# Spreading 24 of 32 expert gathers and sums over the first six head pairs of the next attention

## What is computed

```python
# layer 2: each token goes to its two best experts; their results are weighted and summed
topk_vals, topk_idx = jax.lax.top_k(xf @ router_w.T, 2)
topk_w = jax.nn.softmax(topk_vals, axis=-1)
y = (expert_out_of_each_pair * topk_w).sum(axis=1)
x = x + jnp.tanh(g_ffn[2]) * y
# layer 3: 16 heads over all 512 tokens of a batch, on the normalised x; kv from the context
q_big = rope(einsum(q_hk, w_kc_q)); q_r = einsum(q_big, W_qr); k_r = einsum(rope(kv_c), W_kr)
attn = softmax(q_r k_r^T)            # no scaling
ctx_c = attn @ rope(kv_c); out = (ctx_c @ w_kc_kv^T) @ Wo^T
x = x + jnp.tanh(g_xattn[3]) * out
```

## Time and profile before

| what | us |
|---|---|
| median of 3 runs | 4484.85 (4482.78 to 4489.41) |
| the profiled execution, whole | 4486.73 |
| its span in the trace | 4485.0 |
| PE busy | 3742.6 (83%) |
| DVE busy | 2221.7 (50%) |
| ACT busy | 1204.9 (27%) |
| POOL busy | 363.3 (8%) |

### The profile page before, as it was taken

The page is one execution under the profiler, slowest core; times in us unless marked ns, Lnnn a source line. Parts: engine busy times, 40 slices in busy tenths (PEclk is TensorE's granted clock), DMA queues, the critical chain, the costliest instruction groups (busy, mean ns, idle before and its releaser), DMA issues.

```text
span 4485.0 us, 38317 instructions
## 1 busy us (share of the span) xinstructions
PE 3742.6 (83%) x11794; PEld 1726.6 (38%) x11795; DVE 2221.7 (50%) x3419; ACT 1204.9 (27%) x2333; POOL 363.3 (8%) x388
## 2 busy tenths in 40 slices
PE   2198989884475888937994899999999998999999
PEld 0043434342142444414562344444444443444443
DVE  7787878316365766621113566566665563111111
ACT  1101010013032666612221334434344332001010
POOL 6000000000002222122113000000000000000000
PEclk6599999996786999968997999999999999999999
DMA  2221212130004434234555000000000001222221
GB/s 90 81 75 53 74 56 71 56 123 37 3 0 76 66 50 63 25 142 129 162 164 204 32 32 22 32 32 32 31 22 32 32 22 45 73 80 84 68 87 51
DMA packets 77498, 292.25 MB, mean 65 GB/s; under 512 B 10440, under 2 KB 11336, under 8 KB 66252
## 3 DMA queue, kind: packets, MB, share of 16 engines
q1 hardware_dynamic: 69072, 265.17, 20.1%
q0 software_dynamic: 8320, 25.71, 1.8%
HBM read 256.73 MB, written 33.59 MB: 65 GB/s over the span
## 4 chain that ended last, share of the span: by engine, by line
PE 61%; issue 22%; DVE 7%; DMA 4%; POOL 3%; ACT 2%; SPq 1%; DVEq 0%; POOLq 0%; ACTq 0%
PE BM L338 6%; PE BR L338 6%; PE BS L349 6%; PE BM L1721 5%; PE BM L1772 5%; PE BR L1780 4%; PE BS L1756 3%; PE BM L1731 2%; PE BT L1059 2%; PE BR L1414 2%; PE BM L1403 2%; PE BR L1403 2%; PE BT L1765 2%; PE BM L1745 2%; PE BS L1049 2%
## 5 line engine op out<-in xcount | busy, mean ns | idle before, releaser
L349 PE MATMUL BS<-AR 128*128 128x512 f32 x1024 | 452.8, 595 | 31.9 <-DVE X L393 31.9
L338 PE MATMUL BM<-XT,AR 128*128 (+1 forms) x1024 | 462.8, 595 | 11.9 <-ACT XT L238 5.5
L338 PE MATMUL BR<-XT,AR 128*128 (+1 forms) x1024 | 460.3, 592 | 0.0
L385 DVE TENSOR_TENSOR AR<-AR,BR 128x512 f32<-128x512 f32 x128 | 87.9, 687 | 506.0 <-PE BR L338 494.9
L1944 DVE SCALAR_TENSOR_TENSOR X<-BR,AR,X 128x512 f32<-128x512 f32 x256 | 192.0, 750 | 230.7 <-PE BR L1780 221.4
L1831 ACT COPY AR<-BM 128x512 f32<-128x512 f32 x340 | 199.4, 587 | 397.4 <-PE BM L1772 182.3
L349 PEld LDWEIGHTS BS<-AR 128*128 128x128 f32 x1024 | 191.9, 190 | 287.5 <-issue 229.6
L366 ACT ACTIVATE AR<-BM 128x512 f32<-128x512 f32 x128 | 76.4, 597 | 833.5 <-PE BM L338 833.4
L338 PEld LDWEIGHTS BM<-XT,AR 128*128 128x128 f32 x1024 | 194.5, 191 | 258.3 <-issue 258.3
L338 PEld LDWEIGHTS BR<-XT,AR 128*128 128x128 f32 x1024 | 194.6, 190 | 244.9 <-issue 244.9
L1837 ACT ACTIVATE AR<-BS,AR 128x512 f32<-128x512 f32 x256 | 175.6, 690 | 411.1 <-DVE AR L1931 411.1
(11 more groups left out here) (304 smaller groups left out, 5095.1 us busy)
## 6 DMA issues: line engine op xcount, KB each, us to landing
AR<-l_w_dram SPq DMA_DIRECT2D x128, 512.0 KB, 3.5
AR<-l_wq_dram SPq DMA_DIRECT2D x32, 1152.0 KB, 5.1
AR<-l_w_dram SPq DMA_DIRECT2D x42, 768.0 KB, 4.8
AR<-w2h SPq DMA_DIRECT2D x16, 1024.0 KB, 4.8
QS<-qx SPq DMA_DIRECT2D x32, 512.0 KB, 17.8
AR<-l_w_dram SPq DMA_DIRECT2D x16, 1024.0 KB, 4.8
AR<-l_w_dram SPq DMA_DIRECT2D x8, 1408.0 KB
made<-AR SPq DMA_DIRECT2D x40, 256.0 KB, 4.8
```

What stands on the lines that cost most here:

```text
L338: last = nc.tensor.matmul(bank.rearrange("p (a n) -> p a n", a=1), w[:, kt, a, :], XT[:, ds(b & 1, 1), kt, :], start=kt == 0, stop=kt == K ...
L349: last = nc.tensor.matmul(bank, f.HIDDEN[:, u, st * P:(st + 1) * P], f.DOWN[:, u, :], start=u == 0, stop=u == f.units - 1)
```

## The change

The first four gathers and sums, and the four behind them, stay where they are (k = 0 to 7, batch 0), and POOL issues four more gathers (k = 8 to 11) into the freed buffers ahead of its norm. The gathers k = 12 to 31 go to the beginning of POOL's part of the attention. The sums k = 8 to 31 go into the DVE's loop over pairs, four behind `sums(p)` for p = 0 to 5. To keep the buffers alive the attention's area begins 4 * D columns later, WT0, WT1, YP0 and YP1 get storage of their own, and PROBT3 shrinks to one buffer for both heads; so the context of head 0 moves ahead of the turn of head 1, in the ring's numbering, on PE and on ACT.

```diff
--- before.py
+++ after.py
@@ -1310,8 +1310,10 @@
         EC = a(E + 16 + TW)
         TOK = a(B * ST).bitcast(I32)
         n128 = B * ST * E
-        MX0, MX1, MS, EX, WT0, WT1, POS0, POS1 = [a(B * ST) for _ in range(8)]
-        IDX0, IDX1, YP0, YP1 = [a(B * ST).bitcast(I32) for _ in range(4)]
+        MX0, MX1, MS, EX, POS0, POS1 = [a(B * ST) for _ in range(6)]
+        IDX0, IDX1 = [a(B * ST).bitcast(I32) for _ in range(2)]
+        WT0, WT1 = [sb(n, [P, B * ST])[:, :] for n in ("WT0", "WT1")]
+        YP0, YP1 = [sb(n, [P, B * ST], I32)[:, :] for n in ("YP0", "YP1")]
         NTL, END0, END1, START = a(E), a(E), a(E), a(E)
         EXF = a(TW)
         EXPERT, SLOTS = a(TW).bitcast(I32), a(TW).bitcast(I32)
@@ -1446,6 +1448,21 @@
                     nc.scalar.copy(EHT[:, u, 0:2 * P], bank[:, 0:2 * P])
                     nc.scalar.copy(EHT[0:I - 2 * P, u, 2 * P:], bank[0:I - 2 * P, 2 * P:EK * P]).then_inc(es.free, 1)
 
+        def moe_combine(v, k):
+            tile, j = divmod(k, 2)
+            v.wait_ge(yg_in[k % 4], 16 * (k // 4) + 16)
+            nc.vector.scalar_tensor_tensor(out=X[:, tile, :], in0=YG[k % 4], scalar=(WT0, WT1)[j][:, tile:tile + 1],
+                                           in1=X[:, tile, :], op0=ALU.mult, op1=ALU.add).then_inc(yg_used, 1)
+            v.wait_ge(yg_used, k + 1)
+
+        def moe_gather(pool, k):
+            tile, j = divmod(k, 2)
+            if k >= 4:
+                pool.wait_ge(yg_used, k - 3)
+            nc.gpsimd.indirect_dma_start(out=YG[k % 4], out_offset=None, in_=made,
+                                         in_offset=bass.IndirectOffsetOnAxis(ap=(YP0, YP1)[j][:, tile:tile + 1], axis=0))\
+              .then_inc(yg_in[k % 4], 16)
+
         def moe_vector(v):
             r, m = Count(), Count()
             one = lambda t, n: t.rearrange("p (t o) -> p t o", o=1).to_broadcast([P, B * ST, n])
@@ -1539,12 +1556,8 @@
                     v.wait_ge(y_ready, i * 2 + u + 1)
                     v.sem_inc(er.free, 1)
             l3_context(v)
-            for k in range(2 * B * ST):
-                tile, j = divmod(k, 2)
-                v.wait_ge(yg_in[k % 4], 16 * (k // 4) + 16)
-                nc.vector.scalar_tensor_tensor(out=X[:, tile, :], in0=YG[k % 4], scalar=(WT0, WT1)[j][:, tile:tile + 1],
-                                               in1=X[:, tile, :], op0=ALU.mult, op1=ALU.add).then_inc(yg_used, 1)
-                v.wait_ge(yg_used, k + 1)
+            for k in range(8):
+                moe_combine(v, k)
             v.sem_inc(x_done, B)
             norm_vector(v, 0)
             T_V.step(KT)
@@ -1580,13 +1593,8 @@
                 pool.wait_ge(xg_in[u], (NT // 2 + 1) * 16)
             pool.wait_ge(er.full, ROUTE_R + 2 * NT)
             pool.wait_ge(et.free, NT + 3)
-            for k in range(2 * B * ST):
-                tile, j = divmod(k, 2)
-                if k >= 4:
-                    pool.wait_ge(yg_used, k - 3)
-                nc.gpsimd.indirect_dma_start(out=YG[k % 4], out_offset=None, in_=made,
-                                             in_offset=bass.IndirectOffsetOnAxis(ap=(YP0, YP1)[j][:, tile:tile + 1], axis=0))\
-                  .then_inc(yg_in[k % 4], 16)
+            for k in range(12):
+                moe_gather(pool, k)
             norm_pool(pool)
 
 
@@ -1616,11 +1624,11 @@
         RQ = [a(3, S), a(3, S)]
         QRT = a(S)
         assert a.here() <= E * KT * 2 * I + 2 * EK * D
-        a = area(E * KT * 2 * I + 2 * EK * D)
+        a = area(E * KT * 2 * I + 2 * EK * D + 4 * D)
         MIX = a(3, S)
         QHK, CC3 = [a(S), a(S)], [a(S), a(S)]
         KRT = a(S)
-        PROB3, PROBT3 = [a(ST, S), a(ST, S)], [a(ST, S), a(ST, S)]
+        PROB3, PROBT3 = [a(ST, S), a(ST, S)], a(ST, S)
         SUM3, RS3, NEG3 = [a(2, 2 * ST).rearrange("p u (h s) -> p u h s", h=2) for _ in range(3)]
         KV_TMP = QB.rearrange("p a k n -> p (a k n)").rearrange("p (t c) -> p t c", c=C)
 
@@ -1645,12 +1653,13 @@
                         put("o", "b2", p + 1, h)
                         for k in range(2):
                             put("m", "b", p + 1, h, k)
+                    if p >= 0 and h == 1:
+                        put("m", "ctx", p, 0)
                     if p >= 0:
                         for lt in range(ST):
                             put("t", "turn", p, h, lt)
                 if p >= 0:
-                    for h in range(2):
-                        put("m", "ctx", p, h)
+                    put("m", "ctx", p, 1)
                     if p % 8 == 6:
                         for kt in range(KT):
                             put("t", "norm", p // 8, kt)
@@ -1769,7 +1778,7 @@
                 bank = take(("ctx", p, h))
                 for lt in range(ST):
                     pe.wait_ge(t_free, L3["turn", p, h, lt] + 3)
-                    last = nc.tensor.matmul(bank, KVN[:, p // 8 * ST + lt, :], PROBT3[h][:, lt, :], start=lt == 0, stop=lt == ST - 1)
+                    last = nc.tensor.matmul(bank, KVN[:, p // 8 * ST + lt, :], PROBT3[:, lt, :], start=lt == 0, stop=lt == ST - 1)
                 last.then_inc(m_full, 1)
 
             def outputs(p, h):
@@ -1812,9 +1821,10 @@
                 for h in range(2):
                     if more:
                         big_queries(p + 1, h)
+                    if h:
+                        context(p, 0)
                     turn_probs(p, h)
-                for h in range(2):
-                    context(p, h)
+                context(p, 1)
                 if p % 8 == 6:
                     turn_norm(p // 8)
                 if more:
@@ -1840,7 +1850,7 @@
             def probs(p, h, lt):
                 job = ("turn", p, h, lt)
                 act.wait_ge(t_full, L3[job] + 1)
-                nc.scalar.copy(PROBT3[h][:, lt, :], BT[:, L3[job] % 2, :]).then_inc(t_free, 1)
+                nc.scalar.copy(PROBT3[:, lt, :], BT[:, L3[job] % 2, :]).then_inc(t_free, 1)
 
             def big(p, h, k):
                 if p:
@@ -1880,10 +1890,10 @@
                 if more:
                     for k in range(2):
                         big(p + 1, 1, k)
+                take(("ctx", p, 0), CC3[0])
                 for lt in range(ST):
                     probs(p, 1, lt)
-                for h in range(2):
-                    take(("ctx", p, h), CC3[h])
+                take(("ctx", p, 1), CC3[1])
                 if p % 8 == 6:
                     for kt in range(KT):
                         job = ("norm", p // 8, kt)
@@ -1971,6 +1981,9 @@
                     last = nc.vector.tensor_scalar(XN[:, st, :], X[:, 4 * b + st, :], MV[:, st, 0:1], RSTD[:, st:st + 1], ALU.subtract, ALU.mult)
                 last.then_inc(xn_ready, 1)
 
+            def combine(k):
+                moe_combine(v, k)
+
             v.wait_ge(rope_in, 16)
             for h in range(2):
                 rotate(0, h)
@@ -1984,6 +1997,9 @@
                     for h in range(2):
                         rotate(p + 1, h)
                 sums(p)
+                if 8 + 4 * p < 2 * B * ST:
+                    for k in range(8 + 4 * p, 12 + 4 * p):
+                        combine(k)
                 if p % 8 == 4:
                     norm_begin((p // 8 + 1) % B)
                 if p % 8 == 5:
@@ -1992,6 +2008,8 @@
             add_outputs(NP3 - 1, 1)
 
         def l3_pool(pool):
+            for k in range(12, 2 * B * ST):
+                moe_gather(pool, k)
             for b in range(B):
                 norm_pool(pool)
 
```

## The result

| | before | after |
|---|---|---|
| median of the runs | 4484.61 us (4482.78 to 4489.41, 4 runs) | **4446.2 us** (4444.31 to 4452.07, 4 runs) |
| the profiled execution | 4486.73 | 4444.31 |
| its span | 4485.0 | 4442.6 |

The ratio is 0.9915 with a 95% interval of 0.9898 to 0.9932: 30 to 46 us faster. I had said 4453, between 4447 and 4465. (The runs of experiments 1 and 9 make it ten of this kernel, with a median of 4447.3, so 0.8 us is less than these medians can tell.)

A forecast was written before the change was run, and what follows sets the result against it. PE was taken to stand for XN behind 24 sums that batch 0 does not need. Terms: -34.7 + 0.3 + 3.1 - 1.0 = -32.3 from 4484.85 gives 4452.6, said as 4453, range 4447 to 4465.

The forecast's parts named there:

- The bound: Between experts and last attention, PE waits 31.9 us for XN; with 24 sums moved, PE's own chain comes last instead.
- The norm transposes: PE's turn of XN before the first query matmul: 3.2 us on a busy PE instead of 4.43.
- The weights of pair 0: Their load before the first query: landing at 2424.0 instead of 2428.4 without the gathers, ahead of 2426.0, so no bound.
- The moved sums: DVE in pairs 0 to 5: four sums take 3.11 us of 6.22 idle; only 0.3 us lost, at p = 4.
- crowded-DVE rival: Pairs 0 to 5: sums keep a 1.81 us pace, four take 7.2 us; 6 us lost in all, 4459; 5%.
- The one PROBT3: All pairs: context 0 waits about 0.1 us for its bank, 31 x 0.1 = 3.1 us lost, between 0 and 10.9.
- The slower rivals: PROBT3's single buffer costs 0.35 us a pair (4461, 12%), 0.8 to 1.1 (3%), or 1.8 (4506, 3%).
- The seam held by DMA: Rival before the first query: pair-0 weights land as late as before, start 2428.7, 2.7 us less gain, 4456; 10%.
- The folds: PE's preparation before the KVN transposes: fold loads land in 4.2 us, all later work 1.5 us earlier, at most 2.0.
- The last pair: Context 0 fills PE's 1.36 us wait for the second head's exponentials: 1.0 us gained, between 0 and 2.

The follow-up runs named there:

- experiments 1 and 9: The changed kernel unaltered, run again: 4446.8 us in 1, 2072.0 us from the attention's first load to the end in 9, which also reran before (2107.1 us).
- experiment 6: Changed kernel with eight sums behind each of the first three pairs instead of four behind each of six: median 4476.9 us, ratio 0.9982.
- experiment 3: Changed kernel with the 24 sums in one block behind the norm of batch 0, ahead of the first rotation: median 4471.6 us, ratio 0.9956.
- order-only kernel: Kernel of before with one PROBT3 and context 0 ahead of head 1's turn, gathers and sums unmoved: median 4487.3 us, ratio 1.0004.
- experiment 1: The changed kernel once more, unaltered: median 4446.8 us, ratio 0.9915.

## Why the prediction was right or wrong

Split at S, at the first query, at pair 1's and pair 30's first scores and at the last output, means of two profiles of before and three of the changed kernel:

| stretch (us) | before | after | difference | predicted |
|---|---|---|---|---|
| S to the first query | 83.0 | 47.5 | -35.5 | -34.7 |
| first query to pair 1 | 68.3 | 67.1 | -1.2 | +0.1 |
| pair 1 to pair 30 | 1162.0 | 1164.7 | +2.7 | +3.2 |
| pair 30 to the last output | 83.8 | 80.9 | -2.9 | -0.9 |
| the feed-forward behind it | 710.2 | 710.9 | +0.7 | 0 |
| sum | 2107.2 | 2071.1 | **-36.2** | **-32.3** |

(Each stretch runs from start to start.) The same split by PE's own work, from the windows view, over the stretches where the clock isn't full throughout:

| stretch | PE busy, us | PE idle, us | granted clock |
|---|---|---|---|
| first fold to the first KVN transpose | 22.7, then 19.0 | 9.5, then 10.2 | 0.74, then 0.87 |
| first query to pair 1 | 56.3, then 55.1 | 12.0, then 12.0 | 0.89, then 0.92 |
| pair 30 to the last scores' end | 52.3, then 51.7 | 6.9, then 6.8 | 0.93, then 0.94 |
| from there to the last output's end | 21.2, then 20.2 | 4.0, then 2.8 | 0.86, then 0.93 |

Of the first and the last of these stretches, the rows of the first profiles, before and then after (columns of the earlier trace rows):

```profile
2390.09:2421.57 31.48, 22.16 (x33) 7.87 (x33) 15.02 (x17) 8.78 (x15) 15.99 (x15) 0.76 0.80 278
2383.15:2411.44 28.29, 17.84 (x33) 6.37 (x33) 14.93 (x23) 8.78 (x15) 9.71 (x9) 0.92 0.78 265
...
3750.34:3775.43 25.09, 21.09 (x65) 11.03 (x64) 6.92 (x10) 7.21 (x14) 0.00 (x0) 0.86 0.00 1
3709.03:3732.18 23.15, 20.22 (x65) 10.18 (x64) 6.92 (x10) 6.93 (x14) 0.00 (x0) 0.93 0.00 1
```

**The bound.** Right: PE stood for XN, and won the time when XN came early. What was late next was PE's own chain, as said, with the landing of the pair-0 weights 0.1 us ahead of it in one profile.

**The norm transposes.** Right: 3.15 us measured, 3.2 said.

**The weights of pair 0.** Right: I put their landing at 10.1 us behind the issue; it was 10.8, 9.5 and 12.6, against 14.5 and 14.3 in before.

**The moved sums.** Right: 3.12 us in 6.22, no wait on a gather, 0.3 us lost at pair 4. The crowded-DVE rival falls for four sums, and experiment 6 shows that eight would have cost 8.7 us a pair.

**The one PROBT3.** Right in place and size: 0.085 us a pair, 0.1 said. The slower rivals, 0.35 and 1.1 us a pair or more, fall.

**The seam held by DMA.** Not in the changed kernel, but it was near: in experiment 3 it came true for 2.1 us.

**The step that failed: PE's own time was left at its old lengths in the folds and in the last pair, so both terms were too small.**

- *The folds*: 1.5 us won, at most 2.0. I had one load landing in 4.2 us instead of 5.2, and kept the two folds behind it at their old length ("they take 3.68"), which is the low clock's. Measured: 3.0 us won (2.7 with the order-only kernel counted to before). That load came no sooner on the mean: 5.1 and 4.7 us before, 4.9, 4.0 and 6.2 after. PE's idle time in the folds even grew, from 9.5 to 10.2 us. What shrank was its busy time, 22.7 to 19.0 us, at a clock of 0.87 instead of 0.74; folds 12 and 13 took 1.98 us in all three profiles.
- *The last pair*: 1.0 us won, taken from a wait of 1.36 alone. Measured: 2.2 (2.0 by the order alone), of which 1.2 is the wait and 1.0 is busy time at a clock of 0.93 instead of 0.86: the turn of head 1 took 3.52 us for 16 transposes and takes 1.04 and 1.15 for 8 each. All ten profiles with the new last pair have this clock, and the three with the old one the other. In the same ten the feed-forward behind it takes 0.7 us more, so 1.5 us stay.

Together the two terms put the centre 2.7 us too high. The first pair (1.2) and the last scores (0.7), which I had at nothing, add to that, and the feed-forward takes its 0.7 off again. In the first pair and the last scores the idle time is the same and only the clock differs, and not by the kernel: the first query to pair 1 takes 69.1 and 67.6 us in before, 69.2 in two altered kernels and 65.4 in experiment 1. That part is luck.

**The range** had no room left for it. Its lower end, "down to 35.3 + 2 won, nothing lost, 4447", takes each term at its best and adds nothing for executions of one kernel that differ among themselves, though S alone wanders over 13 us and before ran from 4476.8 to 4493.2 in a later set. The effect from S on, -36.2, would give 4448.4, inside the range; the medians that were compared lie 38.4 apart, and these 2 us are luck too. By that spread I estimate 2 us on either side for a median of four runs.

## What to carry to other kernels

When a block of per-batch work stands ahead of a stage that goes batch by batch, move the norm of the first batch up and feed the rest into idle gaps of its engine, but check both halves: here each was worth some 18 us. Fill a gap only as far as its data have been fetched a turn ahead; a second four sums in each of three pairs lost 25 us, more than the spreading had won. Where a change takes away a wait of PE, look at the granted clock of the rows around it and price the work behind the wait at either level. And compare profiles from an origin just ahead of the change, since the stretch ahead of it moved by more than most of the terms argued about.

## What the runs showed of the hardware

- PE's granted clock in the folds differs between executions of one kernel: groups of two heads in 1.98 us in one profile, of four in 6.49 in the next. It fell behind waits of 2.0 to 4.3 us on a load, but not behind each: after the 3.44 us of the profile of the changed kernel it stayed at 1.00.
- A late engine costs more than its lateness: waits of 6.75 and 7.03 us cost 8.7 us a pair, with the outputs behind them at 3.78 and 3.40 us for four records instead of 1.98.
- Gathers of 256 KB ran at 1.45 us each once the plain loads had landed, the pace of their issue on POOL, and at a mean of 1.81 us in before, partly beside plain loads; holding 20 of them back for 15 us delayed the first query by 3.7.
